# Decoder kernel: context and weights split, first queries, keys and values of the second attention block moved into the end of the first

## What is computed

```python
x = _layernorm(x + _L0_attn_ref(x, wq, wk, wv, wo))             # 16 query heads, 4 key heads of 128, window 64
x = _layernorm(x + _L0_xattn_ref(x, ctx_512, Wq, Wkv_expand, Wout))
...
def _L0_xattn_ref(q, latent_kv, Wq, Wkv_expand, Wout):
    qp = q @ Wq.T                              # from x: 256 features, 16 heads of 16
    k, v = jnp.split(latent_kv @ Wkv_expand.T, 2, axis=-1)   # from the context alone: 64 features
    ...                                        # causal softmax attention
    return out @ Wout.T
```

## Time and profile before

| | us |
|---|---|
| median of 3 runs | 2056.48 (2053.9 to 2057.25) |
| the profiled execution | 2054.35 |
| its span, first to last instruction | 2053.0 |
| TensorE busy | 1820.9 (89%) |
| VectorE busy | 1289.8 (63%) |
| ScalarE busy | 1084.0 (53%) |
| Pool busy | 602.3 (29%) |
| mean granted TensorE clock | 0.942 |

### The profile page before, as it was taken

How to read it: one execution, slowest core, us unless ns; L and a number is a source line. 1 busy time by engine, 2 the same in 40 slices (tenths; PEclk the granted TensorE clock), 3 DMA queues, 4 the chain that set the end, 5 groups by cost and what they waited for, 6 DMA issues and landing times.

```text
span 2053.0 us, 42322 instructions
## 1 busy us (share of the span) xinstructions
PE 1820.9 (89%) x15964; PEld 1538.4 (75%) x15964; DVE 1289.8 (63%) x3373; ACT 1084.0 (53%) x2729; POOL 602.3 (29%) x542
## 2 busy tenths in 40 slices
PE   6988978958986999879999999999999996894995
PEld 6888876744655766679999999999999986673663
DVE  5566555651225555468888888888888886774222
ACT  4656653311212433368888888888888872331221
POOL 5533320022222300234434444444444430003221
PEclk9999998968996999999999999999999997995998
DMA  4000008312229000000000000000000003202233
GB/s 154 11 1 1 1 16 339 107 52 58 47 37 267 19 2 2 21 11 11 11 11 11 26 11 11 11 11 11 11 11 1 1 1 144 114 3 76 37 47 64
DMA packets 51862, 91.72 MB, mean 45 GB/s; under 512 B 4592, under 2 KB 43632, under 8 KB 49232
## 3 DMA queue, kind: packets, MB, share of 16 engines
q1 hardware_dynamic: 42784, 77.64, 11.4%
q0 software_dynamic: 8160, 10.29, 3.2%
q10 hardware_dynamic: 720, 1.09, 0.2%
HBM read 56.13 MB, written 32.87 MB: 43 GB/s over the span
## 4 chain that ended last, share of the span: by engine, by line
PE 70%; DVE 18%; issue 4%; POOL 3%; ACT 3%; DMA 2%; SPq 0%; ACTq 0%; DVEq 0%; POOLq 0%
PE bank L99 58%; PE bank L2293 9%; DVE a_t L630 2%; DVE e_st L2446 2%; DVE e_PT_lo L2465 1%; DVE d_nm L1286 1%; PE bank L1590 1%; DVE a_t L627 1%; PE bank L187 1%; POOL c_rows L1874 1%; POOL g_rows L1874 1%; PE bank L434 1%; DVE f_nm L1286 1%; DVE d_nm L1285 1%; PE bank L1569 1%
## 5 line engine op out<-in xcount | busy, mean ns | idle before, releaser
L2446 DVE TENSOR_REDUCE e_st<-bank 128x1 f32<-128x401 f32 x512 | 291.5, 570 | 143.3 <-PE bank L99 135.7
L2383 ACT ACTIVATE e_P<-bank,e_st 128x400 f32<-128x400 f32 (+1 forms) x512 | 307.1, 600 | 104.9 <-DVE e_st L2450 104.1
L2465 DVE TENSOR_TENSOR e_PT_lo<-bank,e_PT_hi 128x512 fp32r<-128x512 f32 (+1 forms) x448 | 287.9, 643 | 0.0
L2293 PE MATMUL bank<-ident,e_P 128*128 128x128 f32 (+1 forms) x1664 | 260.4, 276 | 17.3 <-DVE e_PT_lo L2465 6.8
L2398 ACT CAST e_PT_hi<-bank 128x512 fp32r<-128x512 f32 (+1 forms) x448 | 248.2, 554 | 26.7 <-PE bank L2293 12.2
L99 PE MATMUL bank<-e_PT_hi,e_kv 128*128 128x256 f32 (+1 forms) x832 | 250.6, 321 | 0.0
L2293 PEld LDWEIGHTS bank<-ident,e_P 128*128 128x128 f32 (+1 forms) x1664 | 196.4, 141 | 53.7 <-issue 38.2
L99 PE MATMUL bank<-e_PT_lo,e_kv 128*128 128x256 f32 (+1 forms) x832 | 217.2, 281 | 0.0
L99 PE MATMUL bank<-e_KT,e_qk_hi 128*128 128x402 f32 x512 | 194.9, 381 | 10.0 <-ACT e_P L2383 6.5
L99 PE MATMUL bank<-e_KT,e_qk_lo 128*128 128x402 f32 x512 | 177.4, 346 | 0.0
L99 PEld LDWEIGHTS bank<-e_PT_lo,e_kv 128*128 128x128 f32 (+1 forms) x832 | 159.6, 192 | 0.0
(11 more groups left out here) (449 smaller groups left out, 4950.8 us busy)
## 6 DMA issues: line engine op xcount, KB each, us to landing
c_wall<-in_c_w SPq DMA_DIRECT2D x8, 1536.0 KB, 18.2
g_wall<-in_g_w SPq DMA_DIRECT2D x8, 1536.0 KB, 18.2
c_rows<-normed SPq DMA_DIRECT2D x9, 1040.0 KB, 12.0
g_rows<-normed SPq DMA_DIRECT2D x9, 1040.0 KB, 13.7
e_stage<-in_e_w SPq DMA_DIRECT2D x16, 416.0 KB, 3.3
c_xs<-c_rows SPq DMA_DIRECT2D x23, 130.0 KB, 2.1
g_xs<-g_rows SPq DMA_DIRECT2D x23, 130.0 KB, 2.1
landing<-in_a_wo SPq DMA_DIRECT2D x2, 1024.0 KB, 6.1
```

Source lines behind the costliest of these rows:

```text
L2293: last = pe.transpose(o[0:rows, c * SEQ + i * P:c * SEQ + (i + 1) * P], p[:, i, k0:k0 + rows], ident[:])
L2383: act.activation(Pm[u % 2][:, i, j * PIECE:j * PIECE + n], bank[score_bank[j]][:, 0:n], ACT.Exp, bias=s[:, i, 4:5], accum_out=s[:, i, j:j ...
L2446: last = dve.tensor_reduce(s[:, i, j:j + 1], bank[score_bank[j]][:, 0:PIECE + 1], AX.X, ALU.max)
L2465: dve.tensor_tensor(lo, bank[tb_bank[at % 2]][0:rows, 0:n * SEQ].rearrange("p (c n) -> p c n", c=n), hi.bitcast(F32), ALU.subtract).then_i ...
```

## The change

A class `Projections` takes over what the second block did for its operands: load and split of the context, split of the weights, and the three projections. An object of it is made before the first block and is handed to both. Its tiles lie in the memory of the first block's key and value weights `a_wkv_hi` and `a_wkv_lo`, which the first block reads last in step 47; therefore the products of the second block's weights have the names `a_wkv` in what follows. The other attention blocks make their own object at their start and behave as before.

In the first block:

- SP loads `ln_w`, `lanes` and the context early, behind the first block's own loads, before it waits to prefetch the block b weights.
- Step 54: ScalarE casts the context. Steps 55 to 57: it casts wq, wk, wv. Steps 55 to 58: VectorE writes the packed context and the three lower halves.
- TensorE projects queries of sequence 0 at the end of step 64 into bank 7, keys (bank 1) and values (bank 3) at the end of step 65.

In the second block SP, ScalarE, VectorE and Pool no longer wait for the last add but for the last output product (`summed.at(N)`, the new `emptied`). TensorE still waits for the add, and then for the keys' evacuation before it writes masks, because the keys are now in bank 1, among the banks of the masks. `gate_scalar()` stays where it is.

```diff
-        def layer0_attention():
+        def layer0_attention(wkv, following):
...
+                OPENED_BESIDE = N - 10
...
+                    sp.dma_start(ln_w[:], t["f_ln"]).then_inc(ln_in, 16)
+                    sp.dma_start(lanes[:], t["lanes"]).then_inc(lanes_in, 16)
+                    sp.wait_ge(*wq_lo.at(2))
+                    following.fetch_context()
                     sp.wait_ge(*wo_lo.at(4))
                     prefetch("b")
...
+                        if i == N:
+                            pe.wait_ge(xt_lo, BATCH - 1)
+                            following.project_q(0, misc)
+                        elif i == N + 1:
+                            pe.wait_ge(*q_cos.at(N // 2))
+                            following.project_k(0, 1)
+                            pe.wait_ge(*exped.at(N))
+                            following.project_v(0, score_bank[1])
...
+                        if i == OPENED_BESIDE:
+                            act.wait_ge(*v_proj.at(2 * BATCH))
+                            following.upper_context()
+                        elif 0 < i - OPENED_BESIDE <= 3:
+                            following.upper(i - OPENED_BESIDE - 1)
...
+                        if i == OPENED_BESIDE + 1:
+                            following.lower_context()
+                        elif 1 < i - OPENED_BESIDE <= 4:
+                            following.lower(i - OPENED_BESIDE - 2)
...
-                return added.at(BATCH)
+                return added.at(BATCH), summed.at(N)
...
+            def fetch_context(self):
+                sp.dma_start(self.ctx_stage, t["ctxT"]).then_inc(*self.ctx_in.up(16))
...
                     if i == FIRST:
-                        return [("q", 0, SIDE), ("k", 0, OUT_BANK), ("v", 0, B_BANK)]
+                        return [("q", 0, SIDE), ("k", 0, 1 if opened else OUT_BANK), ("v", 0, B_BANK)]
...
                 def sync():
-                    sp.wait_ge(*before)
-                    if name == "b":
-                        sp.dma_start(ln_w[:], t["f_ln"]).then_inc(ln_in, 16)
-                        sp.dma_start(lanes[:], t["lanes"]).then_inc(lanes_in, 16)
+                    sp.wait_ge(*emptied)
                     sp.dma_start(wo[:], t[f"{name}_wo"]).then_inc(*wo_in.up(16))
...
                         if i == FIRST:
-                            for x in beside(i):
-                                side(*x)
+                            if opened:
+                                pe.wait_ge(*k_kept.at(1))
+                            else:
+                                for x in beside(i):
+                                    side(*x)
...
-                    act.wait_ge(*before)
-                    if packed_context:
-                        act.dma_start(ctx_stage, t["ctxT"]).then_inc(*ctx_in.up(16))
-                        act.wait_ge(*ctx_in.at(16))
-                        act.copy(ctx_hi[:], ctx_stage).then_inc(*ctx_hi_done.up())
-                    upper(wq[0][:], wq_in)
-                    upper(wk[0][:], wk_in)
-                    upper(wv[0][:], wv_in)
+                    act.wait_ge(*emptied)
+                    if not opened:
+                        if packed_context:
+                            proj.upper_context()
+                        for n in range(3):
+                            proj.upper(n)
                     if routing:
                         routing.gate_scalar()
```

More of the change, by code:

```diff
@@ L260, in layer0_attention @@
                 xT = rows32.rearrange("p n d -> p (n d)")[:, 0:DC * BATCH * SEQ].rearrange("p (c n) -> p c n", c=DC)
-                wkv = [A(f"a_wkv_{s}", [P, DC, 2 * half], F32R) for s in ("hi", "lo")]
                 wq = [A(f"a_wq_{s}", [P, G, DC, REP * HD], F32R) for s in ("hi", "lo")]
@@ L819, in narrow_attention @@
         def narrow_attention(name, block, hd, heads, kv_heads, lane, before, following, carried=(3,), entering=(),
-                             packed_context=None, middle=False, wall=None, routing=None, ahead=None):
+                             packed_context=None, middle=False, wall=None, routing=None, ahead=None, opened=None, emptied=None):
             scale = float(hd) ** -0.5
@@ L827, in narrow_attention @@
             slot = 32 + gap
-            kc = 1 if packed_context else DC
             kvw = kv_heads * hd
+            emptied = emptied or before
             turns_in = 4 * (block - 1)
             turns_out = 4 * block
-            wq_at, wk_at, wv_at = 0, DC * D, DC * D + kc * D
             with ExitStack() as sc:
@@ L835, in A @@
                     return alloc(sc, f"{name}_{n}", *a, **k)
-                wq = [A(f"wq_{x}", [P, DC, D], F32R) for x in ("hi", "lo")]
-                wk = [A(f"wk_{x}", [P, kc, D], F32R) for x in ("hi", "lo")]
-                wv = [A(f"wv_{x}", [P, kc, kvw], F32R) for x in ("hi", "lo")]
+                proj = opened or Projections(sc, name, block, hd, kv_heads, packed_context)
+                w_lo, q_proj, k_proj, v_proj = proj.w_lo, proj.q_proj, proj.k_proj, proj.v_proj
                 wo = A("wo", [P, DC, D])
@@ L956, in tensor @@
                 def tensor():
[L957 to L985, removed]
-                            prods = [x for d in range(kc)
-                                     for x in kv_products(b, d, tok(b), [w[:, d, c * P:(c + 1) * P] for w in wk])]
-                            for n, (r, l) in enumerate(prods):
-                                last = mm(bank[k][:, c * SEQ:(c + 1) * SEQ], l, r, n == 0, n == len(prods) - 1)
-                        last.then_inc(*k_proj.up())
@@ L992, in project_v @@
-                    def project_v(b, k):
-                        pe.wait_ge(*w_lo.at(3))
-                        for i in range(2):
-                            prods = [x for d in range(kc) for x in kv_products(b, d, rows_of(b, i), [w[:, d, :] for w in wv])]
-                            for n, (l, r) in enumerate(prods):
-                                last = mm(bank[k][:, i * kvw:(i + 1) * kvw], l, r, n == 0, n == len(prods) - 1)
-                        last.then_inc(*v_proj.up())
                     def project_out(b, k):
@@ L1168, in scalar @@
                 def scalar():
-                    def upper(dst, src):
-                        act.wait_ge(*landings[name][0].at(16))
-                        act.copy(dst, src).then_inc(*w_hi.up())
                     def keep_q(b, k):
@@ L1260, in vector @@
                 def vector():
-                    def lower(dst, src, hi, n):
-                        dve.wait_ge(*w_hi.at(n))
-                        dve.tensor_tensor(dst, src, hi.bitcast(F32), ALU.subtract).then_inc(*w_lo.up())
                     def keep_q(b, k):
@@ L1335, in norm_part @@
                             norm_vector(b, tiny[b], part)
-                    dve.wait_ge(*before)
-                    if packed_context:
-                        dve.wait_ge(*ctx_hi_done.at(1))
-                        dve.wait_ge(const_in, 48)
-                        dve.scalar_tensor_tensor(ctx_parts[:], ctx_hi[:].bitcast(F32), signs[:, 4:5], ctx_stage,
-                                                 ALU.mult, ALU.add).then_inc(*ctx_packed.up())
-                    lower(wq[1][:], wq_in, wq[0][:], 1)
-                    lower(wk[1][:], wk_in, wk[0][:], 2)
-                    lower(wv[1][:], wv_in, wv[0][:], 3)
+                    dve.wait_ge(*emptied)
+                    if not opened:
+                        if packed_context:
+                            proj.lower_context()
+                        for n in range(3):
+                            proj.lower(n)
                     for i in range(FIRST, LAST + 1):
@@ L1372, in gpsimd @@
                 def gpsimd():
-                    pool.wait_ge(*before)
+                    pool.wait_ge(*emptied)
                     for i in range(2):
```

112 lines of the change are left out of this document (91 added, 21 removed).

## The result

| | before | changed |
|---|---|---|
| median of 20 runs, us | 2055.53 (2053.1 to 2060.04) | 2052.18 (2047.83 to 2057.27) |
| span of the profiled execution, us | 2053.0 | 2050.9 |
| mean granted TensorE clock | 0.942 | 0.942 |

The ratio of the changed kernel to the one before is **0.9982, 95% interval 0.9975 to 0.9989**: 3.7 us or 0.18% faster (2.3 to 5.1 us). A second series of 12 runs gave 0.9978 (0.9966 to 0.9990). So there is a gain, and it is as near to the 0.2% line as forecast. (In the 20 runs of before, three are those known when the forecast was made, with a median of 2056.48.)

The account below looks back on a forecast made before the run. Bound at the border by a chain of loads, splits and the gate's cast, not TensorE. 6.7 - 2.8 + 0.3 = 4.2 us gained, so 2056.48 - 4.2 = 2052.3 us; range 2048.8 to 2055.8.

Parts of the forecast that it names:

- The moved products: Query, key and value products put into the first block's last units: the block ends 0.9 us later.
- The moved splits: Context and weight splits put into units 54 to 58 of the first block: 0.3 us, mostly swallowed by slack.
- The bound of 4.7: Upper bound in us for the moved splits, with all of both engines' split work on the path.
- The wait that takes over: At the border the gate's load, taken as 2.3 us, holds ScalarE's cast and keys; first scores at 307.65, not 314.33.
- The clock: TensorE idles before block b's masks and falls to 1.2 GHz; two pairs of masks and scores give back 2.8 us.
- The clock's return: In block b the clock comes back with the next dense queries, earlier than before; 0.3 us saved, up to 0.55.
- The clock did not stay up (0.22): Rival at block b's first scores: clock stays up or returns at once; 2048.9 or 2050.7 us, chance 0.22.
- The late gate with exposed splits: Rival: gate's load takes 3.14 us and the packing's 1.1 us isn't swallowed; gain about 2.3, 2054.2 us, chance 0.28.
- The slower rival: All splits lie on the path of units 54 to 58, gate late besides; 2057.5 us, chance 0.04.
- the sum: Gain at the border: 6.7 us at full clock, less 2.8 for the slow clock, plus 0.3 for its earlier return.

Follow-up runs that it names:

- late gate experiment: Changed kernel with ScalarE's cast of the expert gate moved behind the first evacuations of keys and values; ratio to before 0.9951, in a later series 0.9967.
- filled wait: Changed kernel with 36 idle products ahead of TensorE's wait for the last add; ratio to the kernel before 0.9964.
- both edits: Changed kernel with the 20 projection products directly behind the first block's last output product and the gate's cast behind the evacuations; ratio to before 0.9963.
- late gate in the kernel before: Kernel before, with only the gate's cast moved behind the evacuations of keys and values; timed once, only its profile used.
- border kernels: Changed kernel with the 20 projection products directly behind the first block's last output product, not in its last units; ratio to before 0.9972.

## Why the prediction held

The forecast was 4.2 us less; the ratio says 3.7 (2.3 to 5.1), and the median 2052.18 lies 0.1 below the forecast of 2052.3, which was worked from a median 1 us higher. That it is 0.1 is luck: the border gained up to 1 us more than forecast (4.6 to 5.3 at the end of block b), and about as much is missing behind it, where the prediction saw no reason for a loss. Step by step:

- **The moved products: 0.9 us forecast, 0.69 measured** (last add at 9.91 against 9.22). Each step came out: from the turn of 292.21 to the values of 293.95 it is 1.74 us, where it was 1.06, so the queries cost the 0.68 forecast; from the turn of 295.31 to the values of 296.59 it is 1.28, where 1.25 was forecast. But the lateness is not handed on whole: that second turn is 0.56 us later than before, counted from unit 63's exponentials, the last values 0.78 (forecast 0.9) and the add 0.69.
- **The moved splits: 0.3 forecast, 0.0 measured** (43.31 against 43.30). The mechanism was right and its slack larger: the packing pushed ScalarE's normalisation by 1.18 us (1.1 forecast), and counted from unit 51's exponentials those of unit 56 start 1.2 us later than before, those of unit 58 0.85, those of unit 59 0.0. The push was swallowed whole. The bound of 4.7 was no exaggeration, though: three units earlier they cost 4.3.
- **The wait that takes over: right.** The gate's load took 2.45 us from its issue to its cast (2.3 forecast), and the late gate experiment shows that it alone held the keys, at a price of 4.1 to 4.8 us at D. The prediction named this as what the change doesn't do. It gave no price for it; part of that price is the clock.
- **The clock: right on the place, right on the size.** Masks 1.01 and scores 3.38, for 0.96 and 3.38 forecast; the filled wait shows that the idle time ahead of the masks was the cause. Its fast first pair (0.61 and 1.95) puts the price of the first pair at 1.83 us, for 1.84 forecast. From the first to the second maxima it is 6.39 us now and was 5.44, 0.95 more, for 0.94 forecast.
- **The clock's return** was to save 0.3. In the three profiles of the changed kernel it came 3.0, 5.9 and 4.7 us after the first query product (316.93 in the first of them), and the third maxima are at 32.99, 34.49 and 33.89, against 38.46 before. So it is a term of chance of 1.5 us, and 0.3 was a guess within it.
- **The rivals.** The clock did not stay up (0.22): it fell 3.6, 3.3 and 2.0 us after the last output product in the three profiles (4.4 before), so the shorter wait was not short enough. The late gate with exposed splits (0.28) was wrong in both halves. The slower rival's mechanism exists, but three units away.

At D the sum made 6.7 - 1.84 = 4.9 against 5.0 to 5.3 measured; after the second pair 3.9 against 4.1 to 4.4. What it was short of there are the 0.2 and 0.3 of the first two points, less 0.15 for the gate's load. The prediction was right up to the border because each link was priced from a row of the same operation in the same state; the time of the whole kernel it also met by luck.

## What to carry to other kernels

When work is moved out of a wait, ask what else the wait was hiding: here a small load that was free before became the last wait, and moving one cast behind what it doesn't concern gave nearly as much again at the border (4.1 to 4.8 us) as the whole change (5.0 to 5.3). Work that keeps TensorE busy in a gap can be worth more at its old place than its own time, since the clock of what follows depends on it. And slack belongs to a unit, not to a loop: the same four pieces cost nothing in one place and 4.3 us three units earlier. Last, follow a gain to the end: what is won at one border can be partly missing behind the next, and one profile of each kernel does not tell.

## What the runs showed of the hardware

- Idle times of TensorE cost a second time. The 4.55 us ahead of the first masks cost 1.83 us more in masks and scores at 1.2 GHz. Behind the first scores every kernel has a wait of 2.05 us but the one that filled it. Where the clock was still up at its start, it fell within the wait (the filled wait, both edits, the late gate in the kernel before) or in the scores behind it (both profiles of before: second scores of 2.84 and 2.87 us); filled with 16 products, it stayed up through the second scores (1.95 us). In the late gate and border kernels it had fallen in the first scores, behind waits of 1.63 and 2.22 us.
- In the changed kernel the clock stayed at 0.50 while masks and 32-row scores kept TensorE busy for 2.00 and 1.92 of 2 us from 304 to 308, and again after the next wait; it rose 3.0 to 5.9 us after the query products began. The Trainium skill (TensorE: Matmul & The Clock Gate, Part 1) says that sustained activity of TensorE releases the throttle. These rows do not bear that out: from 310.22 to 316.0 TensorE has masks, scores and transpositions without a break, and the clock stays where it is:

```profile
310.00:312.00 2.00, 1.78 (x20) 1.59 (x22) 0.16 (x1) 0.00 (x0) 0.00 (x0) 0.50 1.01 430
312.00:314.00 2.00, 1.92 (x17) 1.63 (x15) 0.00 (x0) 0.00 (x0) 0.00 (x0) 0.50 1.00 424
314.00:316.00 2.00, 2.00 (x13) 1.48 (x12) 1.40 (x3) 0.00 (x0) 0.00 (x0) 0.50 1.01 430
```

- Idle products pay here: 28 of them, with results that nobody reads, made the kernel 6.2 us faster by median (2048.84 to 2042.63, 12 and 6 runs of one series), of which the end of block b shows 1.4 to 2.0.
- One program's executions differ by 6 us in a single stretch (54.4 and 60.7 in the changed kernel, from block b's last maxima to block c's first rows), and by 2.7 us before the last unit of the first block (unit 63 starts at 292.42 and 289.72 in the two profiles of the late gate; over all kernels but the one with the earlier splits between 287.5 and 292.4), so stages have to be counted from a mark inside the kernel.
